# Mix products of the last layer on 32 rows each, issued in pairs, with the other products between the pairs

## The reference

```
shifted = pad(x, one token)[:, :T];   delta = shifted - x
low = tanh((x + delta * mu_x) @ W_x1).reshape(B, T, 5, 32)
mus = einsum('blnr,dnr->blnd', low, W_x2) + x_bias
xr, xw, xk, xv, xg = [x + delta * mus[:, :, i] for i in range(5)]
r = xr @ W_r;  k = xk @ W_k;  v = xv @ W_v;  g = xg @ W_g
w = tanh(xw @ W_w1) @ W_w2 + b_w2
```

## Time and profile before

| | |
|---|---|
| median of 3 runs | 1851.65 us (1848.84 to 1853.36) |
| profiled execution, first to last instruction (span) | 1847.4 us |
| mean granted TensorE clock | 0.977 |
| mixing stage, from the first mix product to the last gate product | 1676.69 to 1713.64 us of the span |
| chunk 1, chunk 2, chunk 3 of the stage (from first mix product) | 8.4, 8.4, 7.4 us |
| DVE, ACT and POOL busy, share of the whole span | 78%, 76%, 77% |

### The profile page before, as it was taken

One profiled execution on the slowest core, in us unless ns is written; L12 is line 12 of the kernel. 1 busy time (PEld: TensorE's weight loads), 2 busy tenths in 40 slices (PEclk: granted clock), 3 DMA queues, 4 the chain that ended last, 5 costly groups with the idle time before them and its releaser, 6 DMA issues. The chain is left out here.

```text
span 1847.4 us, 53971 instructions
## 1 busy us (share of the span) xinstructions
PE 1740.1 (94%) x22856; PEld 1101.7 (60%) x22856; DVE 1444.6 (78%) x2658; ACT 1407.5 (76%) x1737; POOL 1430.4 (77%) x851
## 2 busy tenths in 40 slices
PE   5999999999999999999999999986899999978997
PEld 2466666666666666666666666675556666653454
DVE  5888888888888888888888887535988888845785
ACT  2688888888888888888888888943998888853463
POOL 6699999999999999999999999974765566624122
PEclk9899999999999999999999999998999999989998
DMA  5101010111101010101010010050111111110000
GB/s 142 25 20 31 19 31 23 27 26 28 26 24 30 21 31 19 31 23 28 23 31 23 24 26 4 2 165 18 41 40 36 37 37 37 34 26 1 1 0 24
DMA packets 71080, 56.89 MB, mean 31 GB/s; under 512 B 29196, under 2 KB 64184, under 8 KB 70840
## 3 DMA queue, kind: packets, MB, share of 16 engines
q1 hardware_dynamic: 70840, 53.44, 11.5%
HBM read 14.54 MB, written 1.05 MB: 8 GB/s over the span
## 5 line engine op out<-in xcount | busy, mean ns | idle before, releaser
L278 POOL TENSOR_TENSOR ah_probs_lo<-ah_probs,ah_probs_hi 128x1024 f16<-128x1024 f32 x512 | 1072.8, 2132 | 78.8 <-ACT ah_probs L487 78.7
L542 DVE TENSOR_REDUCE ah_part_max<-ah_p_m 128x1 f32<-128x512 f32 x1024 | 669.2, 685 | 120.9 <-PE ah_p_m L342 111.1
L484 ACT ACTIVATE ah_probs_hi<-ah_p_s 128x1024 f16<-128x1024 f32 x512 | 531.2, 1038 | 190.0 <-PE ah_p_s L358 178.8
L487 ACT ACTIVATE ah_probs<-ah_p_s 128x1024 f32<-128x1024 f32 x512 | 532.4, 1040 | 0.0
L372 PE MATMUL ah_p_o<-ah_v_hi,ah_probs_hi 128*128 128x65 f16 x4096 | 470.5, 195 | 5.7 <-POOL ah_probs_lo L278 5.1
L374 PE MATMUL ah_p_o<-ah_v_lo,ah_probs_hi 128*128 128x64 f16 x4096 | 470.5, 193 | 0.0
L376 PE MATMUL ah_p_o<-ah_v_hi,ah_probs_lo 128*128 128x65 f16 x4096 | 470.3, 194 | 0.0
L372 PEld LDWEIGHTS ah_p_o<-ah_v_hi,ah_probs_hi 128*128 128x128 f16 x4096 | 383.0, 98 | 84.3 <-DVE a_attn L565 12.3
L374 PEld LDWEIGHTS ah_p_o<-ah_v_lo,ah_probs_hi 128*128 128x128 f16 x4096 | 378.4, 98 | 91.3
L342 PE MATMUL ah_p_m<-ah_k_hi_lo,ah_q_hi_twice 128*128 128x512 f16 x1024 | 393.9, 385 | 6.6 <-DMA ah_max_q_lo<-ah_lo 3.1
L357 PE MATMUL ah_p_s<-ah_q_hi_twice,ah_k_hi_lo 128*128 128x512 f16 x1024 | 388.6, 379 | 0.8 <-ACT ah_probs L487 0.4
(11 more groups left out here) (316 smaller groups left out, 3090.0 us busy)
## 6 DMA issues: line engine op xcount, KB each, us to landing
ba_v_skew<-ba_v_own SPq DMA_DIRECT2D x64, 129.0 KB, 2.3
ah_q_hi_twice<-ah_hi SPq DMA_DIRECT2D x128, 64.0 KB, 2.0
ah_k_hi_lo<-ah_hi SPq DMA_DIRECT2D x64, 64.0 KB, 1.9
ah_one_k_hi<-ah_hi SPq DMA_DIRECT2D x64, 64.0 KB, 2.0
ah_k_hi_lo<-ah_lo SPq DMA_DIRECT2D x64, 64.0 KB, 2.0
ah_max_q_lo<-ah_lo SPq DMA_DIRECT2D x64, 64.0 KB, 2.0
ah_w_head<-in_w_heads SPq DMA_DIRECT2D x16, 160.0 KB, 2.4
bw_rot<-in_rot SPq DMA_DIRECT2D x4, 512.0 KB, 10.3
```

The lines of the kernel that those rows point to most:

```text
L278: pool.tensor_tensor(pl[:, p % RW, :, :], pb[:, p % RP, :, :], ph[:, p % RW, :, :], ALU.subtract).then_inc(lo_pool, 1)
L484: act.activation(ph[:, p % RW, :, :], p_s[:, p % 2, :, :], ACT.Exp, scale=HD ** -0.5)
L487: act.activation(pb[:, p % RP, :, :], p_s[:, p % 2, :, :], ACT.Exp, scale=HD ** -0.5).then_inc(exp_done, 1)
L542: dve.tensor_reduce(part[:, t, 2 * half + b:2 * half + b + 1], p_m[:, b, :], AX, ALU.max).then_inc(maxed, 1)
```

## The change

`mixes` is cut into calls for some of the five products. Products 0 and 1 are issued as a pair, and so are 2 and 3; a pair waits once, ahead of its first product, for what its second needs. Each product reads its own 32 partitions of `low` and 32 rows of `wx2` (product 4 the first 32 rows of both). `first(c + 1)` now stands between the two pairs, decay between the second pair and product 4, and gate behind product 4.

```
-                def mixes(c):
-                    pe.wait_ge(low_done, 2 * c + 2)
-                    for i in range(MIXES):
-                        n = MIXES * c + i
-                        if n >= 2:
-                            pe.wait_ge(tmp_ready, n - 1)
-                        if n == 1:
-                            pe.wait_ge(lres_done, 1)
-                        low = low_a if i < MIXES - 1 else low_b
-                        pe.matmul(p_kr[:, n % 2, :], wx2[:, i, :], low[:, c % 2, :], start=True,
+                def mixes(c, first_mix, number):
+
+                    last = MIXES * c + first_mix + number - 1
+                    pe.wait_ge(low_done, 2 * c + (2 if first_mix + number == MIXES else 1))
+                    if last >= 2:
+                        pe.wait_ge(tmp_ready, last - 1)
+                    else:
+                        pe.wait_ge(lres_done, 1)
+                    for i in range(first_mix, first_mix + number):
+                        low, rows = (low_a, slice(LR * i, LR * (i + 1))) if i < MIXES - 1 else (low_b, slice(0, LR))
+                        pe.matmul(p_kr[:, (MIXES * c + i) % 2, :], wx2[rows, i, :], low[rows, c % 2, :], start=True,
                                   stop=True).then_inc(mu_ready, 1)
...
                 for c in range(NCH):
-                    mixes(c)
+                    mixes(c, 0, 2)
                     if c + 1 < NCH:
                         first(c + 1)
-                    decay_gate(c)
+                    mixes(c, 2, 2)
+                    decay(c)
+                    mixes(c, MIXES - 1, 1)
+                    gate(c)
```

More of the change, by code:

```diff
@@ L1668, in first, with decay @@
                     pe.matmul(p_y[:, :], wx1[:, P:2 * P], z[:, c % 2, :], start=True, stop=True).then_inc(low_ready, 1)
-                def mixes(c):
-                    pe.wait_ge(low_done, 2 * c + 2)
-                    for i in range(MIXES):
-                        n = MIXES * c + i
-                        if n >= 2:
-                            pe.wait_ge(tmp_ready, n - 1)
-                        if n == 1:
-                            pe.wait_ge(lres_done, 1)
-                        low = low_a if i < MIXES - 1 else low_b
-                        pe.matmul(p_kr[:, n % 2, :], wx2[:, i, :], low[:, c % 2, :], start=True,
+                def mixes(c, first_mix, number):
[8 more added lines that the diff above has]
+                        pe.matmul(p_kr[:, (MIXES * c + i) % 2, :], wx2[rows, i, :], low[rows, c % 2, :], start=True,
                                   stop=True).then_inc(mu_ready, 1)
-                def decay_gate(c):
+                def decay(c):
                     pe.wait_ge(mixed, MIXES * c + W_ + 1)
@@ L1686, in decay_gate, with gate @@
                     pe.matmul(p_w[:, :], ww1[:, :], x_w[:, c % 2, :], start=True, stop=True).then_inc(tw_ready, 1)
+                def gate(c):
                     pe.wait_ge(mixed, MIXES * c + G_ + 1)
```

## The result

| | before | after |
|---|---|---|
| median of 5 runs each | 1851.03 us (1848.26 to 1853.36) | 1865.43 us (1858.37 to 1872.6) |
| ratio, 95% interval | | 1.0094 (1.0067 to 1.0121) |
| profiled execution, span | 1847.4 us | 1870.8 us |
| mean granted TensorE clock | 0.977 | 0.963 |
| stage, first mix product to last gate product | 36.95 us | 56.32 us |

What follows compares the result with a forecast made beforehand. POOL's chain of five adds was taken as the mixing stage's bound; chunk terms +2.1, +1.7, +1.7 and +1.1 summed to +6.6 us, giving 1858.2 us, range 1853.5 to 1862.5.

Steps and rivals of the forecast that it cites:

- rival D: Mixing stage: the TensorE clock falls, giving 1860 to 1870 us, taken as 1866; chance 5%.
- the pair: Mix products on different 32 rows: two overlap in part, holding the array 1.28 us instead of 1.71.
- rival B: Mix pairs: whole pairs run together in 0.86 us, shape changes cost 0.20; +4.4 us, 1856.0; chance 10%.
- the hand sum: Mixing stage, step times added chunk by chunk: +2.1, +1.7, +1.7 and +1.1, together +6.6 us.
- The sign given for a pair: Mix pairs in the profile: through 1.9 us after the start if the forecast holds, 1.45 if fully overlapped, 2.3 if not.
- the forecast's own order of halves: Within a mix pair: one half, two halves together, one half, so 3 x 0.43 = 1.28 us.
- C: Mix pairs: they do not overlap, each takes 1.71 us; +9.6 us, 1861.3; chance 13%.
- Change of shape: PE, switching between 128 and 32 rows six times a chunk: 0.20 us each where PE was running.
- rival A: PE in the mixing stage: changes of array shape cost nothing; +3.7 us, 1855.4; chance 20%.
- Order and waits: Mixing chunks: `first` (1.71) and pair waits delay product 2; POOL idle about 1.2 us ahead of x_k in chunks 1 and 2.
- What bounds the kernel: Mixing stage: POOL's chain of five adds is the bound, 1.05 us a step when fed; PE is only nearly full.
- Rival E: Chunks 1 and 2: PE was the bound, so the change shortens each by up to 0.86 us, to 1850; chance 8%.

Runs made afterwards that it cites:

- e2: Kernel before, old order and waits, with every mix product on its own 32 rows; 1857.53 us, ratio 1.0051.
- e1: Changed kernel with every mix product on all 128 rows, leaving only the new order and pair waits; 1856.57 us, ratio 1.0036.
- e3: Changed kernel plus two constant products on 128 rows ahead of each gate product; 1859.09 us, ratio 1.0046.
- e4: Changed kernel plus two constant products on 32 rows ahead of each gate product; 1871.22 us, ratio 1.011.
- e5: e1 with `first`, decay and gate behind product 4 again, leaving only the pair waits; 1850.12 us, ratio 1.001.
- e9: e6 with two more 128-row constant products between the two pairs of chunk 3; 1851.42 us, ratio 1.0011.
- e7: Kernel before plus four constant products, ahead of `turn_x(1)` and `turn_x(2)`, the wait for weights moved up; 1846.15 us, ratio 0.9985.
- e6: Changed kernel plus two 128-row constant products ahead of each gate product, `turn_x(1)`, `turn_x(2)` and `turn_x(3)`; 1854.25 us, ratio 1.0033.
- e8: e7 with the next chunk's mix product 0 ahead of the gate product and `turn_x(3)` behind chunk 1's mixes; 1840.44 us, ratio 0.9958.
- e10: e8 with every mix product on its own 32 rows, without pairs; 1852.36 us, ratio 1.0013.
- e11: e8 with 32-row mix products issued in pairs; 1851.6 us, ratio 1.002.

## Why the prediction was wrong, step by step

**The step that failed is the granted clock (rival D), for which the sum has no term.** The prediction took the share of time in which PE streams as the measure ("streams 6.9 of 10.1 us a chunk"), doubted D with it, and gave it 5%. What was wrong was the measure. A product on 32 rows counts in that share like one on 128, and for the clock it does not: e2 fell to 0.50 with PE busy 3.79 to 4.00 of 4 us, e1 stayed at 1.00 with 1.99, and e3 and e4 differ by the rows of their fillers alone. The share was not the whole measure for full products either, since e1 and e5 fell at the start of chunk 1, behind waits of PE, with no product on 32 rows in them. No row of the kernel before has f32 products on 32 rows, so the row on the clock and the share in chunk 3 both told of full products only, and the prediction carried them over to another shape without a bound for it. Of after's stage, 56.32 us in the profiled execution, 40.18 are left when the clock is held up (e9): 16.1 us are the clock's. The kernel before has 36.95, of which 1.25 go with e7. The clock's part of the change is thus 14.9 us in that execution. By the medians it is less: e9 is 2.1 us behind before and e7 3.0 ahead, so 5.1 of the 14.4 us are order, waits and shape, and 9.3 the clock's.

D's number, 1866 with 1860 to 1870, is close to the median of 1865.4 in part by luck. It adds 7.8 us of clock to the forecast's 6.6, where the medians have 9.3 and 5.1: the one was too small by nearly as much as the other was too large.

The executions of after scatter with it too, from 1858.37 at a mean clock of 0.971 to 1872.6 at 0.963.

The Trainium skill ("TensorE: Matmul & The Clock Gate", Part 1) has the clock set by how busy PE has been of late. Here e7 agrees, whose fillers hold it at 1.00 in the stage; e2 does not, if busy is what the profile counts, since it runs at 0.50 with PE busy 3.79 to 4.00 of 4 us.

**The term that was mis-sized is the pair.** This alone would not have taken the time out of the range. It holds the array 0.86 us, which is rival B's size; the prediction took 1.28, from an assumed order in which half of one product is queued behind both halves of the other. The Trainium skill's rule on products on different row groups ("TensorE: Matmul & The Clock Gate", Part 3), which the prediction had weighed and set back, gives an estimated 0.86, and the trace agrees with its 1.05 less 0.20. At full clock everything else in the hand sum then comes out: rival B had +1.1 for a chunk with `first`, so 9.5, and e6 shows 9.50 and 9.48; it had +4.4 for the stage, and e9 less e7 is +4.5. Chunk by chunk these are +1.25, +1.10, +1.11 and +1.02 for chunks 0 to 3, where B had +1.3, +1.1, +1.1 and +0.9. The forecast's 10.1 a chunk and +6.6 are too high by this term alone.

The sign given for a pair, through 1.9 us after its start (1.28 + 0.59), was miscounted: the last half starts 0.43 before the 1.28 are over, so the forecast's own order of halves means 1.44. A pair on 128 rows that doesn't overlap at all is through in 1.88 (e1, 1704.53), so by the sign as it stands a kernel without any overlap would have passed for the forecast. The pair of after, with 1.13, rules out C and the forecast's order of halves.

**Change of shape: right, and rival A falls with it.** In e9, from pair A (1699.77) to pair B (1702.75) are 2.98 us; a pair and `first` are 0.86 + 1.71, so 0.40 for two changes, 0.20 each as taken. At 1.2 GHz it is some 0.3 (after: 2.01 from a pair to the next product, less 1.71).

**Order and waits: right in place, and in size at full clock.** The prediction had POOL idle ahead of x_k for 1.2 us with a pair of 1.28; with 0.86 that is 0.8, and in e9 it is 0.76:

```profile
1704.74 1.09 POOL L2020 TENSOR_TENSOR t_x_k<-t_tmp,t_xT_padded 128x512 f32<-128x512 f32 x1 [0.76 <-DVE t_tmp L2089]
```

The price of the order alone, with all rows at 128, is 1.6 a chunk (e1 10.01 against 8.39), half from the pair waits and half from what stands ahead of pair B. In chunk 3 pair B was put 2.85 behind pair A and starts 2.72 behind it in e6. The order also shows what the 32 rows do bring: 10.01 in e1 and 9.50 in e9, so 0.5 a chunk. Two pairs stream 1.7 us less, and the changes of shape take back 0.4 ahead of pair B alone.

**What bounds the kernel: right.** Rival E (PE as the bound) falls: in e1 PE has the same products at the same clock, is busy for only 8.00 of 10.01 us, and the chunk is 1.6 longer. But E's idea was only one step away. When the next chunk's first mix product is moved ahead of the gate product (e8), x_g is no longer waited for and PE becomes the bound in chunk 2, for a gain of 0.32 us there.

**The bounds by which the prediction would be wrong:** it named a POOL gap under 0.3 us, or an end of the stage moved by more than 10 us. The second happened: the last gate product starts 23.5 us later, 19.4 from the stage.

What stays open: the clock was only seen through the granted level of stretches, so how few rows are too few, and whether 64 would do, was not tried, and why e2 holds 1.00 in chunk 2 and not in the others is not explained. Each kernel has one trace, and its executions scatter by several us. Nor is it settled how much of the spread between executions of one kernel comes from the attention part.

## What to carry to other kernels

Before cutting a product to the rows that it needs, ask what else keeps TensorE's clock up around it: a busy PE in the windows does not, if its products use a quarter of the array's rows. In a stage paced by another engine splitting by rows saves little (0.5 us a chunk, e9 against e1) and puts the clock at risk; in the order in which PE is the bound it lost too (e10 and e11 against e8), and no run here shows it to pay. Where PE stands ahead of a chain, look first for a wait that can be moved behind other work, as `turn_x(3)` in e8; full-size products of constants in a gap that stays are worth a trial (e7). Before building on a pair or an order, write its price at full clock and at half clock: here the clock's part was the larger.

## What the hardware showed that was not expected

- Two f32 products on different 32 rows overlap fully: four half records through in 1.13 us, next product 1.05 after the start, where two products on 128 rows take 1.71.
- PE "busy 4.00 of 4.00 us" at a granted clock of 0.50 (e2, 1696 to 1700). The same products with 96 rows of zero weights ran at 1.00 in chunks 1 to 3 of the kernel before: for the clock, rows of zeros had counted.
- The low clock outlasts the 32-row products and is paid by the full ones behind them (e10: 2.07 us for a full product that takes 1.02 at full clock).
- Over the 15 executions of the kernel before that go with e1 to e4, the time goes with the mean granted clock: 1844.5 to 1846 us at 0.981, 1853.8 at 0.973, so some 1.1 us for 0.001. The clock is not all of it: the executions that go with e5 to e8 run from 1846.4 to 1852.1 at one and the same 0.976.
